# The output stage of a two-layer graph kernel, rewritten without engine loops

## The chip, the cores and the metric

The kernel runs on one core of one Trainium2 chip. The metric is the time of one execution in microseconds (us); shorter is better. TensorE is also called PE, VectorE DVE, ScalarE ACT, GpSimd POOL and SyncE SP. SP and POOL issue the DMAs of the stage that is changed.

## The reference

The reference takes 6250 nodes with 256 features and 200,000 edges. A first attention layer and a second, message-passing layer run one after the other; after the second, a node's new row is its old row plus the layer's output, and then a layer norm over 256 features follows:

```
agg = jax.ops.segment_sum(msg, dst, num_segments=x.shape[0])
out = agg @ Wo.T + bo
return x + out                      # x_L1 = _L1(x)
...
x = _layernorm(x + x_L1, axis=-1)   # so 2*x + agg @ Wo.T + bo, normed
```

Only this last part is computed by the stage that the change touches. In it a row of `agg` (the kernel's `sum_tab`, in device memory) is multiplied by the 256x256 matrix `wo`, the bias `bo` and twice the row of x are added, and mean and variance over the row give the scale `rstd` and the offset `shift` of the result.

## The kernel before

The kernel has four stages, each a block of five engine programs that start together and end at a barrier: a projection, the first layer, the edge stage (by far the longest, 2.1 of the 2.65 ms), and `output_stage`. Only `output_stage` differs. All its names carry the prefix o_ in the profile.

Nodes are worked in tiles of 128 rows; there are 50 tiles with the padding (49 hold nodes), in 5 lots of LOT = 10. Each engine has a loop over the lots (`Fori`), and waits on semaphores whose target stands in a register that `Turns` advances once a lot. Within a lot:

- SP loads a tile of sums to `sums[:, j]` (L1273) once TensorE has turned the tile that was there.
- TensorE turns tile j+1 by two transposes into `turned_ps` (L1319, two buffers, one ahead), then multiplies tile j by `wo` in two fp32 products (L1330; the profile shows each as two matmuls).
- ScalarE copies the turned tile from PSUM to `sums_t` (L1346), and between two copies writes one normed tile of the lot before to `result` (L1356).
- VectorE adds the bias (L1384), adds 2x (L1389), takes `bn_stats` (L1394) and `bn_aggr` (L1400). After the tenth tile of a lot, it adds eps (L1403) and inverts (L1405) for all ten tiles at once, ScalarE takes the root (L1350), and VectorE forms `shift` (L1407).
- POOL stores each normed tile (L1286).

The order of the work on each engine is the order in which this code is written; there is no scheduler. What matters at a lot's end is that ScalarE's root stands ahead of all copies of the next lot, and that the root waits for the tenth tile's statistics. The last lot's ten norms stand alone at the end.

Of the kernel before, what the change touches and what calls it, by code (L numbers as in the profile page):

```python
# [92 lines left out]
def gnn_kernel(nc, x, src_tiles, dst_tiles, edge_weight_tiles, src_first, dst_first, attr_groups, n_edges,  # L93
# [16 lines left out]
    with ExitStack() as top:  # L110
# [22 lines left out]
        with nc.cleanup_on_exit(), ExitStack() as ctx:  # L133
# [301 lines left out]
            x_sb=x_sb, ident=ident, wo=wo, bo_rep=bo_rep, sum_tab=sum_tab, out=out, TILES=TILES, LOTS=LOTS, N=N))  # L435
# [802 lines left out]
def output_stage(nc, shared):  # L1238

    x_sb, ident, wo, bo_rep, sum_tab, out, TILES, LOTS, N = (  # L1240
        shared[n] for n in ("x_sb", "ident", "wo", "bo_rep", "sum_tab", "out", "TILES", "LOTS", "N"))
    with nc.cleanup_on_exit(), ExitStack() as ctx:
        scope = Scope(nc, ctx, "o_")
        sb, psum, sem, sems = scope.sb, scope.psum, scope.sem, scope.sems
        sums = sb("sums", [P, LOT, H], F32)
        sums_t = sb("sums_t", [P, 2, 2 * P], F32)
        summed = sb("summed", [P, LOT, H], F32)
        stats = sb("stats", [P, LOT, 6], F32)
        mean_var = sb("mean_var", [P, LOT, 2], F32)
        padded_var = sb("padded_var", [P, LOT], F32)  # L1250
        inverse = sb("inverse", [P, LOT], F32)
        rstd = sb("rstd", [P, LOT], F32)
        shift = sb("shift", [P, LOT], F32)
        result = sb("result", [P, LOT, H], F32)
        turned_ps = psum("turned_ps", [P, 2, 512], F32)
        out_ps = psum("out_ps", [P, 2, 512], F32)

        landed, stored, go = sems("landed", LOT), sems("stored", LOT), sem("go")
        turned, turned_copied, done, biased, sum_ready, stat_ready, result_ready, result_free = (
            sem(n) for n in ("turned", "turned_copied", "done", "biased", "sum_ready", "stat_ready", "result_ready", "result_free"))  # L1260
        var_ready, padded, inverse_ready, rstd_ready, shift_ready = (
            sem(n) for n in ("var_ready", "padded", "inverse_ready", "rstd_ready", "shift_ready"))

        with nc.Block() as block:
            @block.sync
            def _(sp):
                turn = Turns(sp, "sp_o", "tiles_before")
                with sp.Fori(0, LOTS) as lot:
                    for j in range(LOT):
                        reached = turn.reach_before(j)  # L1270
                        sp.wait_ge(go, 1)
                        sp.wait_ge(turned, reached)
                        sp.dma_start(sums[:, j, :], sum_tab[bass.ds(lot * (LOT * P) + j * P, P), :]).then_inc(landed[j], 16)  # L1273
                    turn.step()

            @block.gpsimd
            def _(pool):
                turn = Turns(pool, "pool_o", "now16 tiles")
                pool.sem_inc(go, 1)
                pool.sem_inc(result_free, 2 * LOT)  # L1280

                def store(row, j, rows):
                    reached = turn.reach(j)
                    pool.wait_ge(go, 1)
                    pool.wait_ge(result_ready, reached)
                    pool.dma_start(out[row, :], result[0:rows, j, :]).then_inc(stored[j], 16)  # L1286

                def release(j):
                    pool.wait_ge(stored[j], turn.now16)
                    pool.sem_inc(result_free, 1)  # L1290

                with pool.Fori(0, LOTS - 1) as lot:
                    for j in range(LOT):
                        store(bass.ds(lot * (LOT * P) + j * P, P), j, P)
                        if j >= 3:
                            release(j - 3)
                    for j in range(LOT - 3, LOT):
                        release(j)
                    turn.step()
                for j in range(LOT):  # L1300
                    first = ((LOTS - 1) * LOT + j) * P
                    if first < N:
                        rows = min(P, N - first)
                        store(slice(first, first + rows), j, rows)
                for j in range(LOT):
                    if ((LOTS - 1) * LOT + j) * P < N:
                        pool.wait_ge(stored[j], 16 * LOTS)

            @block.tensor
            def _(pe):  # L1310
                turn = Turns(pe, "pe_o", "now16 tiles tiles_before")
                pe.sem_inc(turned, LOT)
                pe.sem_inc(done, LOT)

                def turn_tile(j):
                    pe.wait_ge(landed[j], turn.now16)
                    wait_slot(pe, turned_copied, j, turn)
                    for k in range(2):
                        last = nc.tensor.transpose(turned_ps[:, j % 2, k * P:(k + 1) * P], sums[:, j, k * P:(k + 1) * P], ident[:])  # L1319
                    last.then_inc(turned, 1)  # L1320

                with pe.Fori(0, LOTS):
                    turn_tile(0)
                    for j in range(LOT):
                        if j + 1 < LOT:
                            turn_tile(j + 1)
                        pe.wait_ge(turned_copied, turn.tile(j))
                        wait_slot(pe, biased, j, turn)
                        for k in range(2):
                            last = nc.tensor.matmul(out_ps[:, j % 2, 0:H], sums_t[:, j % 2, k * P:(k + 1) * P], wo[:, k, :],  # L1330
                                                    start=(k == 0), stop=(k == 1))
                        last.then_inc(done, 1)
                    turn.step()

            @block.scalar
            def _(act):
                turn = Turns(act, "act_o", "now next tiles tiles_before")
                act.sem_inc(turned_copied, LOT)
                act.sem_inc(result_ready, LOT)
                act.sem_inc(rstd_ready, 1)  # L1340
                nc.scalar.preload_act_table(ACT.Sqrt)

                def copy_turned(j):
                    act.wait_ge(turned, turn.tile(j))
                    wait_slot(act, done, j, turn)
                    nc.scalar.copy(sums_t[:, j % 2, :], turned_ps[:, j % 2, 0:H]).then_inc(turned_copied, 1)  # L1346

                def root():
                    act.wait_ge(inverse_ready, turn.next)
                    nc.scalar.activation(rstd[:], inverse[:], ACT.Sqrt).then_inc(rstd_ready, 1)  # L1350

                def norm(j):

                    act.wait_ge(shift_ready, turn.now)
                    act.wait_ge(result_free, turn.tile_before(j))
                    nc.scalar.activation(result[:, j, :], summed[:, j, :], ACT.Identity, bias=shift[:, j:j + 1],  # L1356
                                         scale=rstd[:, j:j + 1]).then_inc(result_ready, 1)

                for j in range(LOT):
                    copy_turned(j)  # L1360
                root()
# [7 lines left out]
                for j in range(LOT):  # L1369
                    norm(j)  # L1370
# [95 lines left out]
```

## Time and profile before

| | us |
|---|---|
| median of 3 runs (lowest, highest) | 2656.9 (2656.55, 2659.18) |
| the profiled execution's own time | 2652.68 |
| its span, first to last instruction | 2651.0 |
| output stage, first DMA issue to the end of the span | 2549.36 to 2651.0 |

The span is 1.7 us shorter than the profiled execution's own time, and that execution was 4.2 us shorter than the median of the runs shown. Over the span TensorE is busy 87% and VectorE 85%, but these shares are those of the edge stage; the output stage has to be read alone. A timeline row gives the start of a group of instructions, its time, the engine and line, what it wrote and read, the count, and in brackets how long the engine had been idle before, and who released it. A row of SPq is the time in which a queue issued DMAs. The end of a TensorE instruction is modelled, so the distance between the starts of two rows is the better measure of its rate. A granted clock of 1.00 is 2.4 GHz, 0.50 is 1.2 GHz.

### The profile page before, as it was taken

How to read it: one execution, taken by the hardware profiler on the slowest of the kernel's cores; microseconds unless marked ns; L12 is line 12 of the kernel's file. 1: busy time of each engine (PE TensorE's matmuls, PEld its weight loads, DVE VectorE, ACT ScalarE, POOL GpSimd, SP SyncE). 2: the span in 40 equal slices, each digit the busy share in tenths (PEclk: the TensorE clock that was granted, in tenths of full speed). 3: DMA queues.
4: the chain of work that ended last, by engine and by line, in shares of the span. 5: the costliest groups of instructions: out<-in, count | busy, mean ns of one | idle time of the engine just before them, and what ended most of it. 6: DMA issues, size and time to landing. Idle time of an engine off the chain costs nothing. (4 is left out here: it accounts for less than half of the span.)

```text
span 2651.0 us, 53452 instructions
## 1 busy us (share of the span) xinstructions
PE 2304.6 (87%) x12356; PEld 1868.8 (70%) x12356; DVE 2257.3 (85%) x6414; ACT 1882.9 (71%) x4004; POOL 1723.8 (65%) x1828
## 2 busy tenths in 40 slices
PE   5436586999999999999999999999999999999975
PEld 4323344877777777777777777878887777778864
DVE  4277566999999999998999999999999999899965
ACT  1234434878788888877888888888888887788844
POOL 3354204777777777777777777777777777777723
PEclk8767788999999999999999999999999999999987
DMA  9646636999999999999999999999999999999943
GB/s 298 190 73 157 183 117 184 279 275 273 267 278 276 278 272 276 276 272 261 272 283 274 269 278 273 284 276 278 279 280 277 277 281 269 264 273 281 281 148 116
DMA packets 318259, 662.33 MB, mean 250 GB/s; under 512 B 79334, under 2 KB 131666, under 8 KB 318224
## 3 DMA queue, kind: packets, MB, share of 16 engines
q0 software_dynamic: 137824, 446.91, 57.6%
q1 hardware_dynamic: 172272, 205.20, 26.3%
q10 hardware_dynamic: 8128, 9.90, 1.2%
q14 instruction: 31, 0.25, 0.0%
q8 instruction: 4, 0.07, 0.0%
HBM read 602.50 MB, written 59.30 MB: 250 GB/s over the span
## 5 line engine op out<-in xcount | busy, mean ns | idle before, releaser
L979 POOL DMA_INDIRECT e_kv<-kv_tab,e_idx x1604 | 1565.3, 976 | 552.8 <-issue 484.7
L1097 ACT ACTIVATE e_gate_ps<-e_gate_ps 128x1024 f32<-128x1024 f32 x802 | 809.9, 1010 | 377.4 <-PE e_gate_ps L1030 377.4
L1159 DVE TENSOR_TENSOR e_gated<-e_kv,e_gate_ps 128x1024 f32<-128x1024 f32 x804 | 973.5, 1211 | 83.7 <-issue 46.6
L1017 PE MATMUL e_sum_ps<-e_gated,e_weighed_hot 128*128 128x256 f32 x3232 | 829.9, 379 | 26.2 <-issue 24.0
L1029 PE MATMUL e_gate_ps<-wd_hi_lo,e_high 128*128 128x512 f32 x1604 | 731.4, 456 | 36.3 <-DVE e_gated L1159 34.6
L1017 PEld LDWEIGHTS e_sum_ps<-e_gated,e_weighed_hot 128*128 128x128 f32 x3232 | 582.7, 189 | 106.9 <-issue 24.8
L1169 DVE CUSTOM_DVE_ANT_0 e_gated<-e_gated,e_q_ps 128x256 f32<-128x256 f32 x1608 | 603.2, 409 | 62.4 <-PE e_q_ps L1049 61.3
L1030 PE MATMUL e_gate_ps<-wd_bias,e_low 128*128 128x512 f32 x1604 | 633.3, 395 | 0.0
L1107 ACT ACTIVATE e_weighed_hot<-e_hot,e_attn 128x128 f32<-128x128 bf16 x1612 | 525.6, 398 | 19.7 <-DVE e_attn L1179 10.6
L1048 PE MATMUL e_q_ps<-e_q_win,e_hot_t 128*128 128x256 f32 x1604 | 405.5, 286 | 69.0 <-issue 68.6
L1049 PE MATMUL e_q_ps<-e_q_win,e_hot_t 128*128 128x256 f32 x1604 | 398.8, 281 | 0.0
L1029 PEld LDWEIGHTS e_gate_ps<-wd_hi_lo,e_high 128*128 128x128 f32 x1604 | 302.3, 188 | 137.0 <-issue 68.0
L1048 PEld LDWEIGHTS e_q_ps<-e_q_win,e_hot_t 128*128 128x128 f32 x1604 | 302.0, 188 | 117.4 <-issue 101.7
L1030 PEld LDWEIGHTS e_gate_ps<-wd_bias,e_low 128*128 128x128 f32 x1604 | 303.7, 189 | 43.2
L1049 PEld LDWEIGHTS e_q_ps<-e_q_win,e_hot_t 128*128 128x128 f32 x1604 | 302.3, 188 | 13.6
L1191 DVE TENSOR_TENSOR e_low<-e_attr,e_high 64x512 fp32r<-64x512 f32 x400 | 271.8, 679 | 1.5 <-ACT e_high L1092 1.5
L1092 ACT CAST e_high<-e_attr 128x512 fp32r<-128x512 f32 x400 | 243.4, 609 | 4.3 <-DMA e_attr<-attr_groups_dram 4.3
L1114 ACT CAST e_hot_t<-e_hot_ps 128x512 fp32r<-128x512 bf16 x400 | 227.0, 568 | 0.0
L1037 PEld LDWEIGHTS e_hot_ps<-ident_bf,e_hot 128*128 128x128 bf16 x1600 | 135.1, 113 | 51.8 <-issue 0.3
L1186 DVE TENSOR_TENSOR e_hot<-iota,e_place 128x512 bf16<-128x512 bf16 x400 | 164.7, 412 | 0.0
L1037 PE MATMUL e_hot_ps<-ident_bf,e_hot 128*128 128x128 bf16 x1600 | 154.6, 219 | 0.0
L1169 DVE DVE_READ_ACCUMULATOR2_ANT e_dot<- 128x1 f32 x1608 | 123.3, 77 | 0.0
(143 smaller groups left out, 1470.0 us busy)
## 6 DMA issues: line engine op xcount, KB each, us to landing
e_attr<-attr_groups_dram SPq DMA_DIRECT2D x800, 128.0 KB
e_kv<-kv_tab,e_idx POOLq DMA_INDIRECT x1604
e_q_win<-q_tab SPq DMA_DIRECT2D x100, 256.0 KB
sum_tab<-e_sums SPq DMA_DIRECT2D x102, 128.0 KB, 4.1
e_prior<-sum_tab SPq DMA_DIRECT2D x101, 128.0 KB
q_tab<-l_q_out SPq DMA_DIRECT2D x50, 256.0 KB, 5.7
kv_tab<-l_kv_out SPq DMA_DIRECT2D x50, 256.0 KB, 6.4
xt_tab<-xt_out SPq DMA_DIRECT2D x50, 132.0 KB, 3.5
```

The lines of the kernel that those rows point to most:

```text
L979: pool.indirect_dma_start(kv[:, k, :], None, kv_tab, bass.IndirectOffsetOnAxis(ap=idx[:, k:k + 1], axis=0)).then_inc(kv_landed[k // G][k % ...
L1017: last = nc.tensor.matmul(sum_ps[:, 0:H], weighed_hot[:, c % 2, k, :], gated[:, c * G + k, H:2 * H], start=(c == 0 and k == 0), stop=(c == ...
L1029: nc.tensor.matmul(gate_ps[:, k, :], high[:, s % 2, cols], wd_hi_lo[:], start=True, stop=False)
L1030: last = nc.tensor.matmul(gate_ps[:, k, :], low[:, s % 2, cols], wd_bias[:], start=False, stop=True)
L1037: last = nc.tensor.transpose(hot_ps[:, k, :], hot[:, c, :, k], ident_bf[:])
L1048: nc.tensor.matmul(q_ps[:, k, :], hot_t[:, s % 2, k, :], q_win[:, 0:H], start=True, stop=False)
L1049: last = nc.tensor.matmul(q_ps[:, k, :], hot_t[:, s % 2, k, :], q_win[:, H:2 * H], start=False, stop=True)
L1097: nc.scalar.activation(gate_ps[:, 2 * p:2 * p + 2, :], gate_ps[:, 2 * p:2 * p + 2, :], ACT.Silu).then_inc(silu_ready[s][p], 1)
L1107: last = nc.scalar.activation(weighed_hot[:, s % 2, k, :], hot[:, s, :, k], ACT.Copy, scale=attn[:, s * G + k:s * G + k + 1])
L1159: nc.vector.tensor_tensor(gated[:, pair(s, p), :], kv[:, pair(s, p), :], gate_ps[:, 2 * p:2 * p + 2, :], ALU.mult).then_inc(gated_ready[s] ...
L1169: last = nc.vector.tensor_tensor_reduce(rows, rows, q_ps[:, k, :], 1.0, 0.0, ALU.mult, ALU.add, dot[:, s * G + k:s * G + k + 1])
L1191: nc.vector.tensor_tensor(low[0:R, c % 2, :], attr[0:R, c, :], high[0:R, c % 2, :], ALU.subtract).then_inc(low_ready[c], 1)
```

## The change

`output_stage` is written without loops for 49 tiles (COUNT), with constants for all waits.

1. All sums are loaded by ten DMAs at the start, in pieces of 1, 1, 2, 4, 8, 8, 8, 8, 8 and 1 tiles, each to its own place in `sums` (49 tiles), on SP. SP then issues the stores too, a tile each, from `sums`, where the norm now writes; POOL has no work in the stage.
2. The bias comes from TensorE: ahead of the two products of a tile stands one fp32r product of 64 rows by 256 columns (L1320), which adds `bo` in two parts (its fp32r rounding and the rest). VectorE's bias addition is gone; it forms 2x plus the product straight from PSUM into `x_sb` (L1368), then `bn_stats` and `bn_aggr`.
3. The norms go by chunks of six tiles: 7 chunks of 6, then 2, 2, 2 and 1. ScalarE makes three copies of the new chunk, takes the root for the chunk before, and then writes two norms for every copy. `sums_t` and `out_ps` have three buffers, and TensorE turns two tiles ahead.
4. ScalarE's table for the root is no longer loaded ahead of the first copy, but ahead of the first root.

The diff, cut to its core:

```diff
+    pieces = cut_up((1, 1, 2, 4, 8))
+    whole = (COUNT - 3) // C
+    chunks = cut_up((C,) * whole + (2,))
...
 # SP
-                with sp.Fori(0, LOTS) as lot:
-                    for j in range(LOT):
-                        reached = turn.reach_before(j)
-                        sp.wait_ge(go, 1)
-                        sp.wait_ge(turned, reached)
-                        sp.dma_start(sums[:, j, :], sum_tab[bass.ds(lot * (LOT * P) + j * P, P), :]).then_inc(landed[j], 16)
+                for i, part in enumerate(pieces):
+                    sp.dma_start(sums[:, span(part), :], ...).then_inc(landed[i], 16)
+                for t in range(COUNT):
+                    rows = min(P, N - t * P)
+                    sp.wait_ge(result_ready, t + 1)
+                    sp.dma_start(out[t * P:t * P + rows, :], sums[0:rows, t, :]).then_inc(stored, 16)
+                sp.wait_ge(stored, 16 * COUNT)
...
 # TensorE
+                def turn_tile(t):
+                    if t in (part[0] for part in pieces):
+                        pe.wait_ge(landed[piece_of[t]], 16)
+                    if t >= 2:
+                        pe.wait_ge(turned_copied, t - 1)
+                    for k in range(2):
+                        last = nc.tensor.transpose(turned_ps[:, t % 2, k * P:(k + 1) * P], sums[:, t, k * P:(k + 1) * P], ident[:])
+                    last.then_inc(turned, 1)
+                turn_tile(0)
+                turn_tile(1)
+                pe.wait_ge(rows_ready, 1)
+                for t in range(COUNT):
+                    if t + 2 < COUNT:
+                        turn_tile(t + 2)
+                    pe.wait_ge(turned_copied, t + 1)
+                    if t >= SLOTS:
+                        pe.wait_ge(sum_ready, t - SLOTS + 1)
+                    nc.tensor.matmul(out_ps[:, t % SLOTS, 0:H], ones_rows[:], bias_rows[:], start=True, stop=False)
+                    for k in range(2):
+                        last = nc.tensor.matmul(out_ps[:, t % SLOTS, 0:H], sums_t[...], wo[:, k, :], start=False, stop=(k == 1))
+                    last.then_inc(done, 1)
...
 # ScalarE
-                nc.scalar.preload_act_table(ACT.Sqrt)
+                for g in range(len(chunks) + 1):
+                    copies = list(chunks[g]) if g < len(chunks) else []
+                    norms = list(chunks[g - 1]) if g else []
+                    for t in copies[:3]:
+                        copy_turned(t)
+                    if g:
+                        root(g - 1)
+                    rest = copies[3:]
+                    while norms or rest:
+                        for t in norms[:2]:
+                            norm(g - 1, t)
+                        for t in rest[:1]:
+                            copy_turned(t)
+                        norms, rest = norms[2:], rest[1:]
...
 # VectorE
-                            nc.vector.tensor_tensor(summed[:, i, :], out_ps[:, i % 2, 0:H], bo_rep[:], ALU.add).then_inc(biased, 1)
+                for g, part in enumerate(chunks):
+                    add_rest(part[0])
+                    if g:
+                        gather_stats(g - 1, chunks[g - 1][-1])
+                        invert(g - 1)
+                    spread(part[0])
+                    for t in part[1:]:
+                        add_rest(t)
+                        if t == part[1] and g:
+                            shifts(g - 1)
+                        gather_stats(g, t - 1)
+                        spread(t)
```

ScalarE around the root, in the kernel before: the end of the loop over the lots. `o_sums_t` is the copy, `o_result` the norm; ISA rows are waits against registers.

```order
L73 ISA x2
L1346 COPY o_sums_t<-o_turned_ps 128x256
L77 ISA
L1356 ACTIVATE o_result<-o_summed,o_shift,o_rstd 128x256
L1350 ACTIVATE o_rstd<-o_inverse 128x10
L90 ISA
L1363 COMPARE_AND_BRANCH
```

ScalarE around a root, in the changed kernel: one chunk of six. The norm now reads `x_sb` and writes `o_sums`.

```order
L1332 COPY o_sums_t<-o_turned_ps 128x256 x4
L1336 ACTIVATE o_rstd<-o_inverse 128x6
L1342 ACTIVATE o_sums<-x_sb,o_shift,o_rstd 128x256 x2
L1332 COPY o_sums_t<-o_turned_ps 128x256
L1342 ACTIVATE o_sums<-x_sb,o_shift,o_rstd 128x256 x2
L1332 COPY o_sums_t<-o_turned_ps 128x256
L1342 ACTIVATE o_sums<-x_sb,o_shift,o_rstd 128x256 x2
```

Three copies of the new chunk moved ahead of the root (the fourth in the first row is the last of the chunk before), and two norms stand ahead of the next copy where one stood.

The same engine in the changed kernel at the end of the program, from the root of the last chunk of six:

```order
L1332 COPY o_sums_t<-o_turned_ps 128x256 x3
L1336 ACTIVATE o_rstd<-o_inverse 128x6
L1342 ACTIVATE o_sums<-x_sb,o_shift,o_rstd 128x256 x6
L1332 COPY o_sums_t<-o_turned_ps 128x256 x2
L1336 ACTIVATE o_rstd<-o_inverse 128x2
L1342 ACTIVATE o_sums<-x_sb,o_shift,o_rstd 128x256 x2
L1332 COPY o_sums_t<-o_turned_ps 128x256 x2
L1336 ACTIVATE o_rstd<-o_inverse 128x2
L1342 ACTIVATE o_sums<-x_sb,o_shift,o_rstd 128x256 x2
L1332 COPY o_sums_t<-o_turned_ps 128x256
```

Here all six norms stand ahead of the next copy, and from then on a root and its norms stand ahead of the copies of every pair.

VectorE in the changed kernel where a chunk begins: `o_padded_var`, `o_inverse` and `o_shift` are those of the chunk before.

```order
L1368 SCALAR_TENSOR_TENSOR x_sb<-x_sb,o_out_ps 128x256
L1377 BN_AGGR o_mean_var<-o_stats 128x2
L1384 TENSOR_SCALAR o_padded_var<-o_mean_var 128x6
L1386 RECIPROCAL o_inverse<-o_padded_var 128x6
L1373 BN_STATS o_stats<-x_sb 128x6
L1368 SCALAR_TENSOR_TENSOR x_sb<-x_sb,o_out_ps 128x256
L1391 SCALAR_TENSOR_TENSOR o_shift<-o_mean_var,o_rstd 128x6
```

In the kernel before these three stood behind the statistics of a lot's tenth tile, with nothing of the next lot beside them; now the new chunk's first addition stands ahead of the inverse, and its second ahead of the shift.

## Rows read from the trace of the kernel before

**Rows 1.** Busy time by stretch (us, count), then clock, DMA share, GB/s.

```profile
2552.50:2569.50 17.00, 14.27 (x64) 11.21 (x64) 11.45 (x42) 3.73 (x10) 0.00 (x0) 0.85 0.53 156
2569.50:2586.00 16.50, 12.79 (x60) 10.49 (x60) 11.81 (x44) 8.81 (x21) 5.47 (x10) 0.90 0.48 159
```

**Rows 2.** Timeline, stage start: start us, us, engine, line, operation, count, [idle before].

```profile
2549.36 18.46 SPq L1273 DMA_DIRECT2D o_sums<-sum_tab  x22
...
2552.54 1.39 PE L1319 MATMUL o_turned_ps<-ident,o_sums 128*128 128x128 f32 x4 [7.86 <-DMA o_sums<-sum_tab]
...
2553.34 0.37 ACT L1346 COPY o_sums_t<-o_turned_ps 128x256 f32<-128x256 f32 x1 [3.00 <-PE o_turned_ps L1319]
...
2553.85 2.07 PE L1330 MATMUL o_out_ps<-wo,o_sums_t 128*128 128x256 f32 x4
```

**Rows 3.** Timeline, one steady tile of the first lot, TensorE and VectorE.

```profile
2559.94 0.38 PE L1319 MATMUL o_turned_ps<-ident,o_sums 128*128 128x128 f32 x2
...
2560.15 1.03 PE L1330 MATMUL o_out_ps<-wo,o_sums_t 128*128 128x256 f32 x4
...
2560.23 0.42 DVE L1384 TENSOR_TENSOR o_summed<-o_out_ps,bo_rep 128x256 f32<-128x256 f32 x1
...
2560.57 0.41 DVE L1389 SCALAR_TENSOR_TENSOR o_summed<-x_sb,o_summed 128x256 f32<-128x256 f32 x1
...
2561.02 0.38 PE L1319 MATMUL o_turned_ps<-ident,o_sums 128*128 128x128 f32 x2
...
2561.32 0.42 DVE L1384 TENSOR_TENSOR o_summed<-o_out_ps,bo_rep 128x256 f32<-128x256 f32 x1
```

**Rows 4.** Timeline, the boundary between the first and the second lot.

```profile
2569.24 0.17 DVE L1403 TENSOR_SCALAR o_padded_var<-o_mean_var 128x10 f32<-128x10 f32 x1
...
2569.45 0.22 DVE L1405 RECIPROCAL o_inverse<-o_padded_var 128x10 f32<-128x10 f32 x1
...
2569.70 0.21 ACT L1350 ACTIVATE o_rstd<-o_inverse 128x10 f32<-128x10 f32 x1 [4.56 <-DVE o_inverse L1405]
...
2570.01 0.37 ACT L1346 COPY o_sums_t<-o_turned_ps 128x256 f32<-128x256 f32 x1
...
2570.28 0.60 ACT L1356 ACTIVATE o_result<-o_summed,o_shift,o_rstd 128x256 f32<-128x256 f32 x1
...
2570.51 1.30 PE L1330 MATMUL o_out_ps<-wo,o_sums_t 128*128 128x256 f32 x4 [3.69 <-ACT o_sums_t L1346]
...
2570.79 0.36 ACT L1346 COPY o_sums_t<-o_turned_ps 128x256 f32<-128x256 f32 x1
```

**Rows 5.** Timeline, the end of the kernel.

```profile
2637.50 5.02 ACT L1356 ACTIVATE o_result<-o_summed,o_shift,o_rstd 128x256 f32<-128x256 f32 x10 [0.32 <-DVE o_shift L1407]
...
2638.67 5.24 POOL L1286 DMA_DIRECT2D out_dram<-o_result  x9 [4.51 <-ACT o_result L1356]
```

**Rows 6.** Timeline, two fp32r products of the edge stage.

```profile
2536.11 0.28 PE L1048 MATMUL e_q_ps<-e_q_win,e_hot_t 128*128 128x256 f32 x1
...
2536.23 0.28 PE L1049 MATMUL e_q_ps<-e_q_win,e_hot_t 128*128 128x256 f32 x1
```

**Rows 7.** Timeline, a table load and the root behind it.

```profile
142.25 1.28 ACT L633 ACT_TABLE_LOAD   x1
...
159.44 0.21 ACT L633 ACTIVATE l_rstd<-l_inverse 128x10 f32<-128x10 f32 x1 [15.90 <-DVE l_inverse L722]
```

**Rows 8.** Timeline, a DMA issued behind a load of 6144 KB.

```profile
19.10 15.45 ACTq L279 DMA_DIRECT2D x_sb<-x_dram  x1
```

**Rows 9.** Busy time by stretch, idle TensorE and its clock.

```profile
2182.00:2184.00 2.00, 0.52 (x4) 0.31 (x3) 1.64 (x4) 2.00 (x6) 1.70 (x2) 1.00 1.03 372
...
1251.20:1253.40 2.20, 0.00 (x0) 0.00 (x0) 1.25 (x3) 0.00 (x0) 1.59 (x3) 1.00 0.98 305
...
1254.00:1257.00 3.00, 3.00 (x12) 2.72 (x12) 2.42 (x8) 2.86 (x7) 2.18 (x3) 0.50 0.83 221
...
2567.00:2570.50 3.50, 0.00 (x0) 0.00 (x0) 2.75 (x13) 0.70 (x3) 0.00 (x0) 1.00 0.24 75
```

More of the change, by code:

```diff
@@ L1277, in _ @@
[L1277 to L1307, printed above, removed]
@@ L1348, in root @@
[L1348 to L1357, printed above, removed]
@@ L1359, in _, with copy_turned @@
-                for j in range(LOT):
-                    copy_turned(j)
-                root()
-                turn.step()
-                with act.Fori(1, LOTS):
-                    for j in range(LOT):
-                        copy_turned(j)
-                        norm(j)
-                    root()
-                    turn.step()
-                for j in range(LOT):
-                    norm(j)
+                def copy_turned(t):
+                    act.wait_ge(turned, t + 1)
+                    if t >= SLOTS:
+                        act.wait_ge(done, t - SLOTS + 1)
+                    nc.scalar.copy(sums_t[:, t % SLOTS, :], turned_ps[:, t % 2, 0:H]).then_inc(turned_copied, 1)
@@ new lines, in root, with norm @@
+                def root(g):
+                    act.wait_ge(inverse_ready, g + 1)
+                    nc.scalar.activation(rstd[:, span(chunks[g])], inverse[:, span(chunks[g])], ACT.Sqrt).then_inc(rstd_ready, 1)
+                def norm(g, t):
+                    if t == chunks[g][0]:
+                        act.wait_ge(shift_ready, g + 1)
+                    nc.scalar.activation(sums[:, t, :], x_sb[:, t, :], ACT.Identity, bias=shift[:, t:t + 1],
+                                         scale=rstd[:, t:t + 1]).then_inc(result_ready, 1)
@@ new lines, in _ @@
+                act.wait_ge(rows_zero, 1)
+                for row in (0, LOW_ROW):
+                    last = nc.scalar.copy(bias_rows[row:row + 1, :], bo_rep[row:row + 1, :])
+                last.then_inc(rows_high, 1)
+                for g in range(len(chunks) + 1):
[12 more added lines that the diff above has]
+                        norms, rest = norms[2:], rest[1:]
@@ new lines, in add_rest, with spread, gather_stats @@
+                def add_rest(t):
+                    dve.wait_ge(done, t + 1)
+                    nc.vector.scalar_tensor_tensor(out=x_sb[:, t, :], in0=x_sb[:, t, :], scalar=2.0, in1=out_ps[:, t % SLOTS, 0:H],
+                                                   op0=ALU.mult, op1=ALU.add).then_inc(sum_ready, 1)
+                def spread(t):
+                    dve.wait_ge(sum_ready, t + 1)
+                    nc.vector.bn_stats(stats[:, t, :], x_sb[:, t, :]).then_inc(stat_ready, 1)
+                def gather_stats(g, t):
+                    dve.wait_ge(stat_ready, t + 1)
+                    last = nc.vector.bn_aggr(mean_var[:, t, :], stats[:, t, :])
+                    if t == chunks[g][-1]:
+                        last.then_inc(var_ready, 1)
@@ new lines, in invert, with shifts @@
+                def invert(g):
+                    cols = span(chunks[g])
+                    dve.wait_ge(var_ready, g + 1)
+                    nc.vector.tensor_scalar(padded_var[:, cols], mean_var[:, cols, 1], EPS, None, ALU.add).then_inc(padded, 1)
+                    dve.wait_ge(padded, g + 1)
+                    nc.vector.reciprocal(inverse[:, cols], padded_var[:, cols]).then_inc(inverse_ready, 1)
+                def shifts(g):
+                    cols = span(chunks[g])
+                    dve.wait_ge(rstd_ready, g + 1)
+                    nc.vector.scalar_tensor_tensor(out=shift[:, cols], in0=mean_var[:, cols, 0], scalar=-1.0, in1=rstd[:, cols],
+                                                   op0=ALU.mult, op1=ALU.mult).then_inc(shift_ready, 1)
```

131 lines of the change are left out of this document (51 added, 80 removed).

## The prediction

> **What bounds the kernel now.** I read the table of stretches first, then timelines of the output stage. Everything before 2549.36 us is unchanged, so only the last 102 us of the span count. A lot of ten tiles takes about 17 us, and in it TensorE is busy 14.3 and 12.8 us, VectorE 11.5 and 11.8, ScalarE 8.8 [rows 1]: nobody is full, so there is a gap in each lot. Inside a lot, tiles follow each other every 1.08 to 1.09 us. On TensorE a tile is a pair of transposes (0.21 from start to start) and the products (0.87), 1.08 together; on VectorE the bias addition comes back after 1.09 [rows 3]. So the two engines are equally full in a lot's steady part, and making only one of them lighter gains nothing there. The gap is the lot's end: eps at 2569.24, inverse at 2569.45, root at 2569.70, the first copy at 2570.01, and TensorE, idle for 3.69 us, starts at 2570.51 [rows 4]. With the slow clock behind it the loss is 17 less 10.9, some 6 us a lot. At the very end ten norms run alone, 5.02 us, and POOL's nine stores behind them take 5.24 and end at 2643.91 [rows 5]; the span ends 7.1 us later at 2651.0.
>
> **TensorE's work for a tile.** It keeps 1.08 us and gets one fp32r product of 256 columns. Two such products in the edge stage start 0.12 apart [rows 6], so a tile becomes 1.20. The bounds are 0 (its time wholly beside the weight loads) and 0.43 (half of the 0.87 that two fp32 products take [rows 3]); I take 0.12, the row with the same type and width. At half clock I take the double: the first products of the stage took 2.07 against 1.03 later [rows 2, 3], so a tile costs 2.4.
>
> **VectorE's work for a tile.** The bias addition (0.34 to the next start [rows 3]) goes. What stays is 0.34 for the addition, which may be followed by its dependent `bn_stats` 0.1 later, and some 0.4 for the statistics: about 0.85. It is no longer at the limit; TensorE alone is, at 1.20, which is slower than the 1.09 of before.
>
> **The start.** TensorE's first transposes come at 2552.54, 3.2 us after SP's first issue [rows 2]; I leave both where they are. The zeros, ones and bias rows (five small VectorE and two ScalarE instructions, under 2.5 us by the 0.4 of their larger kin [rows 3]) lie inside these 3.2 us. A mean clock of 0.85 over the first 17.0 us [rows 1] means 5.1 us at half clock, to 2557.6. In them go the first two tiles' transposes (1.39 [rows 2]), those of the third, which wait for the first copy (2553.34, 0.37 long, and 0.13 to TensorE's start, as at 2570.51 [rows 2, 4]), and one tile's products with the bias, to 3.85; half of the next tile's 2.4 fits too. The product of tile 6 is then done at 2552.5 + 5.7 + 5 x 1.20 + 0.2 = 2564.4. The table load costs nothing: the one at 142.25 ran while its root still waited, to 159.44 [rows 7], and here it lies in the wait for the first inverse.
>
> **A chunk of six, the step that decides.** Let D be the moment when the chunk's first product is done. VectorE: addition at D+0.13, `bn_aggr` at 0.47, eps at 0.66, inverse at 0.87 (spacing 0.21 [rows 4]). ScalarE's root at 1.12 (0.25 behind the inverse [rows 4]). The shift stands behind the second tile's addition, which starts at 1.38 (its product is done at 1.20), so it runs 1.72 to 1.89, and the first norm starts at 2.00. Norms alone follow each other by (5.02 - 0.60)/9 = 0.49 [rows 4, 5], a copy starts 0.51 behind a norm and a norm 0.27 behind a copy [rows 4]. Two norms, and then the copy of the chunk's fourth tile: 3.00 to 3.37. TensorE could have turned the chunk's sixth tile at 2.2 (D-0.2 and two tiles), but that transposition needs the buffer which this copy empties: it starts at 3.5, and refilling costs 0.1. The next two copies, each behind two norms, come at 4.27 and 5.54 and hold TensorE by 0.1 in all; then three tiles run free. The next D is at 3.6 + 4 x 1.20 + 0.2 = 8.6, against 7.2 for six tiles without a stall. Six such periods lead from tile 6 to tile 42: 51.6 us. Before, 36 tiles took 36/10 of 17, 61 us.
>
> **The end.** From the product of tile 42 (D = 0) six norms stand ahead of the copy of tile 44: 2.0 + 6 x 0.49 = 4.9, TensorE restarts at 5.4, product done at 6.8. A new round of addition, statistics, inverse, root and shift (2.0) and two norms (1.0) gives copy 46 at 9.8 and its product at 11.6; another gives copy 48 at 14.5 and its product at 16.1; the norms of 46 and 47 follow at 17.7 and 18.2, the last root at 18.7, the last norm 19.3 to 19.9. TensorE idles 4, then over 2, then over 2 us here. As it loses its clock after such gaps (below), I add 3.0, between 0 and the 4.5 of all four tiles at half clock. So 22.9.
>
> **Loads and stores.** 6.3 MB of loads now stand in one queue ahead of all stores. A DMA issued behind 6144 KB held its issuer 15.45 us [rows 8], so I take the loads as gone at about 2568, the first store as wanted at 2567, and the 49 stores as caught up long before the end; tiles land faster than one in 1.20 us. Nothing waits for this: cost 0, up to 1 us. POOL's pace (9 stores in 5.24, 0.58 each against 0.49 for a norm [rows 5]) leaves the end, already in the next line.
>
> **Sum.** 2564.4 + 51.6 + 22.9 = 2638.9 for the last norm; 0.5 for the issue of the last store and the same 7.1 behind it: 2646.5. Against the span of 2651.0 that is 4.5 us less, and the same 4.5 off the profiled execution (2652.68). The median of the runs shown lies 4.2 above that execution; I take the difference over to it: 2656.9 - 4.5 = 2652.4.
>
> **What the skill says.** At the loop's branch the copy starts 0.10 behind the root's end [rows 4], so I gave the removed branches nothing. The Trainium skill (Runtime: NRT & Kernel Launch, Instruction fetch mechanics) says that a taken branch out of the fetched window stalls an engine until code arrives, and that unrolling avoids it; by it the five lots would give something back here. The trace doesn't bear that out at this branch.
>
> **The rivals.** (a) No stall: ScalarE gets its copies out in time and TensorE's 1.20 sets the pace. For it: a copy and a norm take only 0.78 [rows 4]. Against it: the order of the code, in which two norms always stand before the fourth copy. It would give 6 x 1.4 = 8.4 more, 2644.0. (b) Slower: TensorE's clock falls in every chunk's stall. Between lots it fell after an idle 3.7 us, and in the edge stage a wholly idle 2.20 was followed by 3.00 at 0.50, while a stretch with 0.52 of 2.00 busy stayed at 1.00 [rows 9]. The stall here is 1.4 long, nearer the last. If it fell each time for 3.0 us as there, 1.5 us were lost in each of six chunks, 9 in all: 2661.4. It decides from about one fall in two. Another place of the Trainium skill (TensorE: Matmul & The Clock Gate, HAM oscillation) describes a kernel whose pauses for data put every burst back to the half clock; by that rule (b) would hold, and the trace agrees for the pauses at a lot's end. (c) The bias product costs as much as half of the fp32 pair, 0.43: 0.31 more for each of about 35 tiles that TensorE paces, 11 us: 2663. (d) The small chain on VectorE and ScalarE takes longer than the 2.0, by up to 0.5 in nine rounds: 2657.
>
> **How the numbers follow.** The forecast 0.58, with 2648 to 2656 as its own range; (a), in whole or in good part, 0.22; (b) 0.08, (c) 0.04, (d) 0.08. The range runs from just under (a) to just under (b): 2643 to 2660. A measurement of this kernel tells 0.2%, 5.3 us, from no change, and my 4.5 lies just inside. So the forecast gives faster 0.25, same 0.32, slower 0.01; (a) gives faster 0.21, same 0.01; (b), (c) and (d) give same 0.08, slower 0.12. Together faster 0.46, same 0.41, slower 0.13.
>
> **What would show it.** In the changed profile the new product starts 0.12 ahead of the next one, and steady tiles lie 1.20 apart. TensorE idles a good 1 us once in six tiles, released by a copy, in the pair of transposes of a chunk's sixth tile; the clock stays 1.00 from 2558 to about 2616. The last norm starts near 2638. I am wrong if the stall is missing, if the clock falls inside the chunks, or if the last seven tiles take far from 23 us.

## The result, and the profile after

| | before | after |
|---|---|---|
| median of 7 runs on one chip (lowest, highest), us | 2659.18 (2653.34, 2661.48) | 2668.6 (2663.59, 2675.4) |
| profiled execution, its span, us | 2652.68, 2651.0 | 2665.41, 2663.7 |
| output stage, from SP's first issue to the end | 101.6 | 113.8 |

The changed kernel is slower: the ratio is 1.0038 (1.0024 to 1.0053), and the prediction (2652.4, range 2643 to 2660) was wrong. The stage alone grew by 12.2 us between these two profiles (by 10.5 between a second pair, before_again and after_again below). What was forecast wrong is TensorE's work for a tile, and it is seen best in the steady part. This is the timeline of TensorE's products and then of its weight loads (PEld) over one steady tile of the changed kernel, the answer to [rows 3]:

```profile
2568.06 0.38 PE L1308 MATMUL o_turned_ps<-ident,o_sums 128*128 128x128 f32 x2
2568.37 0.38 PE L1320 MATMUL o_out_ps<-o_bias_rows,o_ones_rows 64*128 64x256 f32 x1
2568.68 1.13 PE L1322 MATMUL o_out_ps<-wo,o_sums_t 128*128 128x256 f32 x4
2569.65 0.38 PE L1308 MATMUL o_turned_ps<-ident,o_sums 128*128 128x128 f32 x2
...
2568.37 0.18 PEld L1320 LDWEIGHTS o_out_ps<-o_bias_rows,o_ones_rows 64*128 64x128 f32 x1 [0.17 <-issue]
2568.68 0.73 PEld L1322 LDWEIGHTS o_out_ps<-wo,o_sums_t 128*128 128x128 f32 x4
2569.44 0.36 PEld L1308 LDWEIGHTS o_turned_ps<-ident,o_sums 128*128 128x128 f32 x2
```

From start to start: transposes 0.31 (0.21 before), bias product 0.31, products 0.97 (0.87 before), together 1.59 us where 1.20 was forecast and 1.08 stood before. The new product costs 0.51, not 0.12: 0.31 of its own and 0.10 on each neighbour. The weight rows show how. The weights of the bias product start to load at 2568.37, when the product itself starts, and those of the product behind it at 2568.68, again with it; the transpose's load (2569.44) runs 0.21 ahead of its product. Ahead of the load of the 64-row weights the loading side stands idle for 0.17, with "issue" as the reason: nothing that the profile shows held it. The same in the groups of the whole stage (count, busy time and mean ns of one, then idle time before them):

```profile
L1308 PE MATMUL o_turned_ps<-ident,o_sums 128*128 128x128 f32 x98 | 21.3, 305 | 16.5 <-DMA o_sums<-sum_tab 8.3 <-ACT o_sums_t L1332 8.2
L1320 PE MATMUL o_out_ps<-o_bias_rows,o_ones_rows 64*128 64x256 f32 x49 | 20.3, 414 | 2.0 <-ACT o_sums_t L1332 2.0
...
L1320 PEld LDWEIGHTS o_out_ps<-o_bias_rows,o_ones_rows 64*128 64x128 f32 x49 | 9.8, 199 | 12.2 <-issue 9.7 <-ACT o_sums_t L1332 2.5
```

The chunk's small chain and its stall, in the timeline of the changed kernel (the answer to [rows 4]; columns as there):

```profile
2571.45 0.42 DVE L1368 SCALAR_TENSOR_TENSOR x_sb<-x_sb,o_out_ps 128x256 f32<-128x256 f32 x1 [0.71 <-PE o_out_ps L1322]
...
2571.99 0.17 DVE L1384 TENSOR_SCALAR o_padded_var<-o_mean_var 128x6 f32<-128x6 f32 x1
2572.20 0.19 DVE L1386 RECIPROCAL o_inverse<-o_padded_var 128x6 f32<-128x6 f32 x1
...
2572.43 0.21 ACT L1336 ACTIVATE o_rstd<-o_inverse 128x6 f32<-128x6 f32 x1 [0.68 <-DVE o_inverse L1386]
...
2573.38 0.16 DVE L1391 SCALAR_TENSOR_TENSOR o_shift<-o_mean_var,o_rstd 128x6 f32<-128x6 f32 x1
...
2573.57 1.09 ACT L1342 ACTIVATE o_sums<-x_sb,o_shift,o_rstd 128x256 f32<-128x256 f32 x2 [0.94 <-DVE o_shift L1391]
...
2574.57 0.35 ACT L1332 COPY o_sums_t<-o_turned_ps 128x256 f32<-128x256 f32 x1
...
2574.97 0.44 PE L1308 MATMUL o_turned_ps<-ident,o_sums 128*128 128x128 f32 x2 [0.38 <-ACT o_sums_t L1332]
```

Addition, eps, inverse, root, shift, two norms, copy, TensorE: the order and the wait are the forecast ones. The next chunk's addition comes at 2581.59, 10.14 us behind this one: six tiles of 1.59 and a stall of 0.60. The table was loaded at 2570.46 (1.28 long), ahead of the first root, in ScalarE's idle time.

The end of ScalarE's work and TensorE's restarts, the answer to [rows 5]:

```profile
2634.42 3.06 ACT L1342 ACTIVATE o_sums<-x_sb,o_shift,o_rstd 128x256 f32<-128x256 f32 x6 [0.94 <-DVE o_shift L1391]
2637.38 0.62 ACT L1332 COPY o_sums_t<-o_turned_ps 128x256 f32<-128x256 f32 x2
...
2657.90 0.60 ACT L1342 ACTIVATE o_sums<-x_sb,o_shift,o_rstd 128x256 f32<-128x256 f32 x1 [0.23 <-DVE o_shift L1391]
```

```profile
2637.78 0.69 PE L1308 MATMUL o_turned_ps<-ident,o_sums 128*128 128x128 f32 x2 [3.94 <-ACT o_sums_t L1332]
...
2645.98 0.66 PE L1308 MATMUL o_turned_ps<-ident,o_sums 128*128 128x128 f32 x2 [2.06 <-ACT o_sums_t L1332]
...
2653.45 0.38 PE L1320 MATMUL o_out_ps<-o_bias_rows,o_ones_rows 64*128 64x256 f32 x1 [1.96 <-ACT o_sums_t L1332]
```

And busy time by stretch in the changed kernel (stretch, length, then PE, PEld, DVE, ACT, POOL; granted clock, DMA share, GB/s), the answer to [rows 1, 9]:

```profile
2552.50:2560.00 7.50, 5.83 (x16) 3.78 (x17) 0.85 (x2) 1.49 (x4) 0.00 (x0) 0.50 0.88 301
2560.00:2565.50 5.50, 5.50 (x15) 3.55 (x14) 1.76 (x6) 0.74 (x2) 0.00 (x0) 0.50 1.09 385
2565.75:2637.25 71.50, 65.84 (x284) 45.63 (x282) 38.35 (x144) 35.48 (x88) 0.00 (x0) 1.00 0.27 96
2637.50:2650.90 13.40, 11.06 (x25) 6.83 (x26) 3.23 (x14) 2.52 (x8) 0.00 (x0) 0.50 0.13 47
```

The clock is 1.00 from 2565.75 to 2637.25, with the stalls of all the chunks in it, and 0.50 ahead of that and behind it, but for 3.4 us near the end (tile 48's products at 2653.45 run at the full clock). At the start TensorE is 5.50 of 5.50 us busy in the second stretch and still at 0.50.

In numbers, counted from SP's first issue of the stage (us; "128 rows" is the first experiment):

| | before | forecast | after | 128 rows |
|---|---|---|---|---|
| VectorE's addition of tile 6 | 14.1 | 15.2 | 21.6 | 16.1 |
| of tile 42, six chunks later | 77.1 | 66.8 | 82.4 | 65.9 |
| end of the last norm | 93.2 | 89.5 | 108.6 | 87.1 |
| end of the span | 101.6 | 97.1 | 113.8 | 92.4 |

Against the kernel before, the 36 tiles in the middle are no slower, since the gaps between lots are gone: 60.8 us against 62.9 (60.5 in before_again). What makes the changed kernel the slower one are its two ends, 7.4 us more to tile 6 and 6.9 more behind tile 42 (4.6 and 5.6 in the second pair of profiles). Against the forecast all three parts are too long.

### The profile page after: what moved, and what is told of

It reads as the page before. It is cut to its first block and busy times, and to the rows that moved or that the text cites. A ratio compares the mean times of both kernels' runs of the same rounds, so it can differ in the third digit from the quotient of the medians.

```text
span 2663.7 us, 52425 instructions
## 1 busy us (share of the span) xinstructions
PE 2330.6 (87%) x12399; PEld 1873.4 (70%) x12399; DVE 2247.5 (84%) x6384; ACT 1882.7 (71%) x4010; POOL 1699.7 (64%) x1779
## 5 line engine op out<-in xcount | busy, mean ns | idle before, releaser
L1017 PE MATMUL e_sum_ps<-e_gated,e_weighed_hot 128*128 128x256 f32 x3232 | 829.3, 379 | 26.2 <-issue 24.0
L1107 ACT ACTIVATE e_weighed_hot<-e_hot,e_attn 128x128 f32<-128x128 bf16 x1612 | 525.7, 398 | 18.8 <-DVE e_attn L1179 9.7
L1037 PEld LDWEIGHTS e_hot_ps<-ident_bf,e_hot 128*128 128x128 bf16 x1600 | 135.0, 113 | 51.6
```

The source lines that it names most:

```text
L1017: last = nc.tensor.matmul(sum_ps[:, 0:H], weighed_hot[:, c % 2, k, :], gated[:, c * G + k, H:2 * H], start=(c == 0 and k == 0), stop=(c == ...
L1037: last = nc.tensor.transpose(hot_ps[:, k, :], hot[:, c, :, k], ident_bf[:])
L1107: last = nc.scalar.activation(weighed_hot[:, s % 2, k, :], hot[:, s, :, k], ACT.Copy, scale=attn[:, s * G + k:s * G + k + 1])
```

## Experiments

Two theories stood for the 0.51. **R, rows:** a product of 64 rows between products of 128 rows cannot have its weights loaded ahead, nor can the product behind it. **F, format:** it is the switch between fp32 and fp32r that breaks the stream. R says that 128 rows cure it, F that fp32 cures it. Some of the expectations also ask about a theory **C, clock:** that the 64-row product keeps TensorE at the half clock longer at the stage's start. The edits of the two operands that make the bias product:

```
BIAS_ROWS = 64      # rows128: 128   (ones_rows and bias_rows have so many rows, all but two of them zero)
bias_rows = sb("bias_rows", [BIAS_ROWS, H], F32R)     # fp32_64: F32
ones_rows = sb("ones_rows", [BIAS_ROWS, P], F32R)     # fp32_64: F32
```

The chip on which the first four ran took some 1000 us more for the stages ahead of this one (kernel before: median 3643.26 of 25 runs, 3624.59 to 3670.64), with a wider scatter. Ratios say less there, so these four are judged by the output stage in their profiles.

**128 rows** (rows128)

> The changed kernel with the bias product over 128 rows instead of 64 (the further rows are zero), still fp32r. In the changed kernel a steady tile took 1.59 us on TensorE instead of the 1.20 I had predicted: the bias product's weights are loaded only when the transposes are through, 0.31 us before the next product starts. Theory R (rows): weights for 64 rows can't be loaded ahead beside work on 128 rows; then a steady tile falls to 1.20 us, a chunk of six from 10.14 to 8.6, and the time by some 12 us or more to about 2654. Theory F (format): one fp32r product between fp32 ones costs this; then 1.59 stays, within 0.05, and so does the time, 2668.

Measured: stage 92.4, steady tile 1.20 to 1.21, chunk 8.3; median 3639.59, ratio 0.9997 (0.9964 to 1.0029). Its timeline, weight loads and products by start:

```profile
3573.90 0.35 PEld L1308 LDWEIGHTS o_turned_ps<-ident,o_sums 128*128 128x128 f32 x2
3574.11 0.38 PE L1308 MATMUL o_turned_ps<-ident,o_sums 128*128 128x128 f32 x2
3574.22 0.19 PEld L1320 LDWEIGHTS o_out_ps<-o_bias_rows,o_ones_rows 128*128 128x128 f32 x1
3574.25 0.37 PE L1320 MATMUL o_out_ps<-o_bias_rows,o_ones_rows 128*128 128x256 f32 x1
3574.34 0.75 PEld L1322 LDWEIGHTS o_out_ps<-wo,o_sums_t 128*128 128x128 f32 x4
3574.46 1.03 PE L1322 MATMUL o_out_ps<-wo,o_sums_t 128*128 128x256 f32 x4
...
3575.32 0.38 PE L1308 MATMUL o_turned_ps<-ident,o_sums 128*128 128x128 f32 x2
```

Twice the rows, all of the added ones zero, and the tile is 0.39 us shorter (3574.11 to 3575.32 is 1.21). The products' weights now load 0.12 ahead (3574.34 against 3574.46) and the bias product's own 0.03 ahead (3574.22 against 3574.25), with no idle time on the loading side, and the steady rate is the forecast one. This is R's number.

**fp32 with 64 rows** (fp32_64)

> The changed kernel with the bias product in fp32 instead of fp32r, still 64 rows. It streams as two matmuls, 0.43 us. Theory F (format): the gaps around it go, a steady tile takes 1.08 + 0.43 = 1.51 us. Theory R (rows): the gaps stay, a steady tile takes about 1.59 - 0.11 + 0.43 = 1.9 us, and the time rises by some 15 us to 2683.

Measured: stage 133.0, steady tile 1.90 to 1.91; median 3687.31, ratio 1.0158 (1.0107 to 1.0209). Without any change of format both loads still wait:

```profile
3571.07 0.73 PEld L1322 LDWEIGHTS o_out_ps<-wo,o_sums_t 128*128 128x128 f32 x4 [0.33 <-issue]
3571.82 0.36 PEld L1308 LDWEIGHTS o_turned_ps<-ident,o_sums 128*128 128x128 f32 x2
3572.34 0.29 PEld L1320 LDWEIGHTS o_out_ps<-o_bias_rows,o_ones_rows 64*128 64x128 f32 x2 [0.17 <-issue]
```

F falls. In fp32 the bias product is two 64-row matmuls, one right behind the other, and windows cut to the second alone show its load and the matmul itself:

```profile
3572.45 0.19 PEld L1320 LDWEIGHTS o_out_ps<-o_bias_rows,o_ones_rows 64*128 64x128 f32 x1
3572.67 0.38 PE L1320 MATMUL o_out_ps<-o_bias_rows,o_ones_rows 64*128 64x256 f32 x1
```

The second load runs 0.22 ahead. So between two matmuls of 64 rows the load does go ahead; only where 64 rows follow 128, and 128 follow 64, does it wait.

**No bias product** (no_bias): L1320 is taken out and the first product starts the sum; the output bias is missing from the result.

> The changed kernel with the bias product left out: the output bias is missing from the result. All else stays. It prices the product whole. Expected by both theories: a steady tile 1.08 us, a chunk of six 3.6 + 4 x 1.08 + 0.2 = 8.1 us instead of 10.14 (the predicted stall behind the fourth copy grows from 0.6 to 1.6 us and eats part of the gain). Theory C (clock): the product also holds TensorE at the half clock longer, since from 2553.6 to 2565.6 the changed kernel ran at 0.50 although TensorE looks busy; then here the clock is full within about 5 us of the first transposition, and the last seven tiles get faster too. With C the time falls by 12 + 5 + 3 = 20 us to 2649; without C by 13 us to 2656.

Measured: stage 89.8, steady tile 1.08 to 1.09, chunk 8.0; median 3646.15, ratio 0.9995 (0.9957 to 1.0033). So the 128-row product costs 0.12 a tile, as forecast, and 2.6 us in the stage; the 64-row product costs 24.0 (113.8 less 89.8), or 20.3 by the second profile of the changed kernel (110.1). The clock was full 7.75 us after the first transposition, not after the 5 that C gave.

**Four copies ahead of the root** (four_first)

```diff
-                    for t in copies[:3]:
+                    for t in copies[:4]:
...
-                    rest = copies[3:]
+                    rest = copies[4:]
```

> The changed kernel with four copies instead of three ahead of each root on ScalarE. The predicted stall, TensorE waiting for the copy of a chunk's fourth tile, should vanish: a chunk takes 6 x 1.59 = 9.54 us instead of 10.14, and TensorE has no wait for a copy inside the full chunks. Over seven chunks 4 us less, 2664; the rival is that the fourth copy holds the root up, since it waits for a tile that is turned later, and moves the stall to the shift: 10.1 stays.

Measured: chunk 9.56, six even tiles of 1.59; stage 110.2; median 3659.68, ratio 1.0047 (1.0022 to 1.0071). The stall is gone and 0.58 per chunk with it, about its length. What bounds a chunk is then TensorE's 1.59 alone. Only the chunk tells this: the stage's 110.2 is no shorter than the changed kernel's second profile (110.1), and the ratio no better.

The next four ran on a chip with the usual times (kernel before: median 2654.61 of 17 runs, 2646.76 to 2660.84).

**The kernel before again** (before_again)

> The kernel before, profiled beside the others, since the last four ran where the edge stage takes about 1 ms longer. What counts from here on is the output stage, from SP's first load issue to the end of the span. Expected 101.6 us as in the first profile, within 3 us; if it is far from that, the stage lengths of the other runs can't be set against the first two profiles.

Measured: 2653.01, stage 99.6, against 101.6 in the first profile; the stage of one kernel varies by some 2 us.

**A version without the stall and without the 64 rows** (stream128): 128 rows, and ScalarE's copies are no longer bound to their chunk.

```diff
-                    for t in copies[:3]:
-                        copy_turned(t)
+                    if g < len(chunks):
+                        copy_to(chunks[g][0] + 4)     # all copies up to the new chunk's fourth
...
-                            for t in rest[:1]:
-                                copy_turned(t)
+                            copy_to(copied + 1)       # the next one, of whichever chunk
```

> The bias product over 128 rows, and ScalarE's copies run ahead of the norms: four tiles beyond a chunk's first before its root, and one copy after every two norms also in the last chunks. All prices are now known: 1.20 us a tile, no stall. First product at the place of rows128; 16 us to tile 6, 43.3 to tile 42, 7.3 to tile 48, some 4 for the last small round, 5.2 behind the last norm: stage 76 us, against 92.4 of rows128 and 101.6 of the kernel before. If the tail's small rounds don't depend on the copies but on the chain through VectorE and ScalarE, it stays near 84.

Measured: median 2628.67, ratio 0.9897 (0.9863 to 0.993), stage 75.6, steady tile 1.20 to 1.21. TensorE, by stretch (columns as above), is full and at full clock:

```profile
2562.00:2614.00 52.00, 51.84 (x300) 44.71 (x300) 39.75 (x152) 35.41 (x89) 0.00 (x0) 1.00 0.46 160
```

It beats both kernels. The rounds of copy, product and statistics at the end are gone too: from the addition of tile 42 to the last norm's end 11.5 us, where the changed kernel took 26.2.

**The same order, the bias by POOL** (stream_pool): no bias product; POOL adds half the bias to x ahead of VectorE's doubling.

```diff
+                for t in range(COUNT):
+                    nc.gpsimd.tensor_tensor(x_sb[:, t, :], x_sb[:, t, :], half_bo[:], ALU.add).then_inc(prepared, 1)
```

> As the last, but with no bias product: POOL, which has no work in this stage, adds half of the bias to each tile of x ahead, so that twice x brings it whole. If POOL needs under 1.08 us a tile and VectorE keeps its pace, a tile takes 1.08 and the stage 71 us. If POOL needs more than 1.2 us a tile, or slows VectorE beside it, it is no faster than stream128, 76 us or more.

Measured: median 2648.61, ratio 0.998 (0.9967 to 0.9994), stage 94.7. A miss. TensorE's tile was the expected 1.08 only where it didn't wait for a copy by ScalarE (1.25 where it did), and VectorE's timeline has the same instruction on 128x6 elements twice, first short, then of this length:

```profile
2569.99 0.27 DVE L1390 TENSOR_SCALAR o_padded_var<-o_mean_var 128x6 f32<-128x6 f32 x1
...
2578.21 18.63 DVE L1390 TENSOR_SCALAR o_padded_var<-o_mean_var 128x6 f32<-128x6 f32 x1
2596.88 0.19 DVE L1392 RECIPROCAL o_inverse<-o_padded_var 128x6 f32<-128x6 f32 x1
```

and POOL's beside it:

```profile
2569.50 27.32 POOL L1304 TENSOR_TENSOR x_sb<-x_sb,o_half_bo 128x256 f32<-128x256 f32 x40
```

VectorE's instruction ended at 2596.84, POOL's unbroken run at 2596.82. The Trainium skill (SBUF — State Buffer, SBUF: two separate sides) says that VectorE and GpSimd share a pair of ports under an exclusive lock, held for one instruction, and that some VectorE operations need it. The two ends agree with a loser that stops altogether, but the wait was not one POOL instruction (0.69 us): it was the 27 that were left. The same instruction at 2569.99, in the same unbroken run of POOL, took only 0.27. That the ports are the cause is read from the two ends, not tested, and what decides between 0.27 and 18.63 stays open. Less the 18.6 us the stage is 76.1, close to stream128's 75.6; TensorE also worked at half clock for 5 us behind the stop, so an estimate without it lies somewhat lower.

**The bias by VectorE, two tiles ahead** (bias_vector): no bias product, otherwise the changed kernel.

```diff
+                def prepare(t):
+                    nc.vector.scalar_tensor_tensor(out=x_sb[:, t, :], in0=x_sb[:, t, :], scalar=2.0, in1=bo_rep[:],
+                                                   op0=ALU.mult, op1=ALU.add).then_inc(prepared, 1)
```

> Only the bias part undone: no bias product, VectorE adds the bias (into x, two tiles ahead), the rest is the changed kernel. VectorE then has four instructions a tile again, some 1.15 to 1.20 us with the dependent one behind the addition. A chunk of six takes 8.3 to 8.8 us, the stage 93 us, 21 less than the changed kernel's 113.8 and about 8 less than before. If VectorE's fourth instruction delays the chain from a chunk's first product to its root, the chunk takes over 9 and the stage nearly 100.

Measured: median 2642.75, ratio 0.9948 (0.9928 to 0.9968), stage 93.9, chunk 8.4. TensorE now idles 1.35 us for a copy in every chunk, and the clock (last but two in the row, columns as above) stays full over all of them:

```profile
2558.80:2620.00 61.20, 48.66 (x252) 37.31 (x252) 49.61 (x189) 36.57 (x91) 0.00 (x0) 1.00 0.39 138
```

With the bias back on VectorE the rest of the change is a gain: 0.5% faster than before, where the whole change was 0.4% slower.

The last four ran beside a kernel before with a median of 2660.05 (9 runs, 2650.68 to 2671.02).

**fp32 with 128 rows** (fp32_128)

> The changed kernel with the bias product in fp32 over 128 rows: the fourth corner beside the changed kernel (fp32r, 64), rows128 (fp32r, 128) and fp32_64. Theory R: no gaps, a steady tile takes 1.08 + 0.43 = 1.51 us, 0.4 less than fp32_64 although it does more. Theory C (clock: 64-row products keep TensorE at half clock longer): the clock is full within 10 us of the first transposition, as in all kernels without 64-row products so far, against 21.5 us in fp32_64. If format and rows both count, the tile takes more than 1.6.

Measured (one run): 2673.01, steady tile 1.52, stage 104.8. The stage is shorter than the changed kernel's and the time longer, because the stages ahead, which are the same, took 14 us more here (the stage began at 2566.5, in after_again at 2552.7). The clock was full after 8.5 us, as C expected. It completes the table of the steady tile:

| us a tile | 128 rows | 64 rows |
|---|---|---|
| fp32r | 1.20 | 1.59 |
| fp32 | 1.52 | 1.90 |

Without the product it is 1.08. 64 rows cost 0.38 or 0.39 in either format, fp32 costs 0.31 or 0.32 with either number of rows: two causes that don't touch each other. In fp32 there are two 64-row matmuls in a tile and in fp32r one, and both pay 0.38 or 0.39: what is paid for is the pair of changes, from 128 rows to 64 and back, not each matmul of 64 rows.

**The changed kernel again** (after_again)

> The changed kernel once more, for the clock alone. The steady tile (1.59) and the chunk (10.1) should repeat to 0.02 us. By theory C the clock is again full only some 10 us or more behind the first transposition (12.5 the first time), and the last seven tiles again take about 26 us; if the first profile was an odd one, it is full after 5 to 8 us and the stage is some 5 us shorter than 113.8.

Measured (one run): 2664.48, stage 110.1, steady tile 1.59, chunk 10.1. The clock was full after 10.0 us and the last seven tiles took 25.2: less than the first time (12.5 and 26.2), more than "an odd first profile" would give. The stage of one kernel thus differs by up to 3.7 us between two profiles, 2.7 of them in its start.

**The streaming order with 64 rows** (stream64)

> stream128 with the 64-row bias product again: ScalarE's order alone is changed. A tile takes 1.59 without a stall: 21.5 us to tile 6, 57.3 to tile 42, 9.5 to tile 48, 4 and 5.2 behind: stage 97.5 us, against 113.8 and 75.6. So the order alone would bring it just under the kernel before, and the rows alone further. If it takes over 105 us, the two parts are not separate.

Measured (one run): 2648.04, stage 93.9, tiles 1.59 without a stall. Between it and stream128 lie 18.3 us of stage; 48 tiles by 0.39 are 18.7. So the rows cost the same in this order too. It was 3.6 us shorter than expected, 2.7 of them in the start (18.8 to tile 6, not 21.5).

**The streaming order with the bias on VectorE** (stream_vector)

> Bias on VectorE as in bias_vector and ScalarE's copies ahead as in stream128. TensorE has 1.08 us a tile, but VectorE about 1.15 and 0.4 to 0.5 more a chunk: 1.2 us a tile, stage 76 us, no better than stream128 by more than 2 us. If VectorE holds 1.08, it is 71 us.

Measured: median 2633.24 (6 runs), ratio 0.991 (0.9882 to 0.9939), stage 75.8. TensorE's tile is 1.08 where it doesn't wait, but the additions are 1.06 to 1.50 apart, on average (58.2 - 13.9)/36 = 1.23. Between the additions of tile 6 and tile 42 VectorE is busy 42.5 of 44.2 us and hardly ever waits for TensorE (0.2 us in all): it now has its limit just where TensorE had it in stream128. The two can't be told apart by their ratios.

## Why the prediction was wrong, step by step

- **TensorE's work for a tile: the step that failed.** It read "It keeps 1.08 us and gets one fp32r product of 256 columns ... so a tile becomes 1.20", by the row with the same type and width [rows 6]. Those products had 128 rows, the new one 64. It costs 0.51, beyond even the bound of 0.43, for the bound too looked only at a product's own time and not at the loads on both sides. With 128 rows it costs the 0.12. Rival (c), a dearer bias product, named the right term with a chance of 0.04, but priced it at 0.43, and for another reason.
- **VectorE's work:** right. It waits for TensorE in every tile, 0.71 in a steady one and 0.35 behind the small chain; 1.59 less 0.71 is 0.88, where 0.85 was forecast.
- **The start:** tile 6 came 6.4 late (3.7 in after_again). The clock was 0.50 for 12.5 us from the first transposes (10.0), not 5.1, and a tile costs 2.94 at that clock, not 2.4. With 128 rows the term was 0.9 off.
- **A chunk of six:** the mechanism was right, the first norm 2.12 behind the addition's start where 1.87 was forecast (the shift waits behind the second tile's addition, which now comes 1.59 later). Its price was another: TensorE is slower and arrives later at the copy, so the stall is 0.60 instead of 1.4 (0.60 is what the chunk's 10.14 has beyond six tiles of 1.59). 36 tiles by 0.39 less 6 stalls by 0.8 are 9.2, and 60.8 stand against 51.6. With 128 rows the period is 8.3 against 8.6.
- **The end:** from tile 42's addition to the last norm 26.2 for 22.8. The idle times were as forecast (3.94, 2.06, 1.96 against 4, over 2, over 2), the tiles between them dearer, most of them at half clock. With 128 rows it is 21.2.
- **Loads and stores:** right. Behind the first load TensorE waited for one more, 0.61 us ahead of the third tile's transposes (2555.28), inside the allowance of 1 us. Behind the last norm it took 5.2 us, not 7.6. It is 5.2 in every version that stores by SP, whose last store is issued within 0.4 us of the last norm's end, and 8.5 and 8.7 in the two profiles of the kernel before, which stores by POOL; the forecast had carried the 7.1 behind POOL's last store over to SP. Why it is shorter behind SP's wasn't tested.
- **Rival (a)** did not come; four_first shows what it would have been worth, 0.58 a chunk. **Rival (b)** is refuted: the clock is 1.00 over 71.5 us with all stalls in it. These stalls are shorter than its 1.4, but in bias_vector TensorE idles 1.35 six times and the clock stays at 1.00 too. The rule that the prediction set beside (b) was drawn too wide: it fits the idle 3.69 at a lot's end, and no idle time of 1.35 or less lowered the clock here. **Rival (d)**, a longer small chain, came in half: 0.25 more in a full chunk (2.12 for 1.87) as a follower of the longer tile, for with 128 rows the chain took 1.74.

The misses add up: 6.4 + 9.2 + 3.4 - 2.4 = 16.6 of the 16.7 by which the stage is longer than forecast. How much of it the 64 rows explain is shown by rows128: 21.4 us in the stage, 5.5 in the start, 11.0 in the chunks and 5.0 at the end. With after_again in place of the first profile it is 17.7, and the difference lies in the start and the end; the 11.0 in the chunks repeats. Without them the change makes the stage 92.4, 7 to 9 us shorter than before, a little more than the forecast 4.5.

Why a change of height holds the loads up is only read, not tested. The Trainium skill (TensorE: Matmul & The Clock Gate, The mechanism) says that a weight load overlaps a running product only when their row groups differ, or when it goes to the background buffer. The runs show that loads between products of equal height do overlap, with 128 rows and, in fp32_64, with 64 (0.22 ahead), and that it is the change of height that ends it. The same page (Why this matters for your kernels) has a single product with few rows take the time of a full one. That holds for the product's own record (0.38 us with 64 rows, 0.37 with 128) and misleads here: 0.39 of the 0.51 come with the wait of the loads. Two 64-row matmuls in a row pay it once, 0.38 (fp32_64 against fp32_128); longer runs of them were not tried.

## What to carry to other kernels

Price an added TensorE product by a row of the same height, not only the same type and width, and look at the weight loads of both neighbours; if it has fewer rows than the 128-row products around it, pad it with zero rows. When a tuned loop is rewritten, look for what each engine is ordered behind: letting copies run ahead of the chunk brought 17 us here (92.4 to 75.6; 16 to 20 with 64 rows, 110.1 or 113.8 to 93.9), more than the 7 to 9 of the whole change with 128 rows. A new wait is worth its length only if the engine would have been early; here a slower TensorE hid more than half of it (0.60 for 1.4).

## What the runs showed of the hardware

- A 64-row fp32r product of 256 columns between 128-row products: 0.51 us a tile; with 128 rows 0.12. Two fp32 matmuls of 64 rows together: 0.82; with 128 rows 0.44. The change of height costs 0.38 or 0.39 whether one or two 64-row matmuls stand between.
- A VectorE tensor_scalar on 128x6 fp32 elements held 18.63 us, until POOL's row of tensor_tensor ended; in the same row of POOL's work one took 0.27.
- Six idle times of 1.35 us on TensorE, 8.4 us apart, left its clock at 1.00 (bias_vector); the idle 3.94 of the changed kernel's end was followed by work at 0.50.
- TensorE's clock at the stage's start stayed at 0.50, counted from the first transposes in steps of 0.25 us, for 5.25 to 9.5 us in the six profiles without a bias product, 7.25 to 8.5 in the three with 128 rows, and 7.75 to 21.5 in the five with 64 rows (21.5 in fp32_64). The four longest are all with 64 rows, but the ranges overlap, and one kernel had 12.5 and 10.0 in two profiles; theory C is neither shown nor refuted, and what decides it stays open.
